# Four stages' starts and attention's score banks in one graph transformer kernel

## The reference, cut to what matters

```python
x = x + gnn0(ln(x), adj)      # 8 heads of 16: softmax(mask(n n^T / 4)) n, then an MLP 128 -> 512 -> 128
x = x + ffn0(ln(x))           # slice attention: 64 slices per head, attention among them, and back
x = x + gnn1(ln(x), adj)      # two graph convolutions: root and relation weights, divided by the degree, elu
x = x + ffn1(ln(x))           # shared expert, plus the best 2 of 8 experts per token

# gnn0, per graph
normed = layer_norm(x, gamma1, beta1)
qkv = normed.reshape(b_, n_, H, HD).transpose(0, 2, 1, 3)
scores = jnp.einsum('bhqd,bhkd->bhqk', qkv, qkv) * scale
attn = jax.nn.softmax(jnp.where(adj_matrix[:, None, :, :] > 0, scores, -jnp.inf), axis=-1)
out = jnp.einsum('bhqk,bhkd->bhqd', attn, qkv)
```

## Time and profile before

| | us |
|---|---|
| median of 3 runs | 2728.17 (2725.9 to 2731.24) |
| the profiled execution, and its span | 2732.5, 2730.6 |
| TensorE busy | 2636.5 (97%) |
| VectorE, GpSimd, ScalarE busy | 1928.5, 1499.3, 1471.2 (71%, 55%, 54%) |
| attention, MLP, slice attention, graph stage, experts | 536.5, 237.5, 762, 538.5, 656.5 |

### The profile page before, as it was taken

How to read it: one execution, slowest core, us unless ns; L and a number is a source line. 1 busy time by engine, 2 the same in 40 slices (tenths; PEclk the granted TensorE clock), 3 DMA queues, 4 the chain that set the end, 5 groups by cost and what they waited for, 6 DMA issues and landing times. The chain is left out here.

```text
span 2730.6 us, 85746 instructions
## 1 busy us (share of the span) xinstructions
PE 2636.5 (97%) x28783; PEld 2141.0 (78%) x28784; DVE 1928.5 (71%) x6630; ACT 1471.2 (54%) x2930; POOL 1499.3 (55%) x2542
## 2 busy tenths in 40 slices
PE   8999999899989999999999899899998999999999
PEld 4666666589968888888888677777788999999888
DVE  5777777567779999999999588777864544555453
ACT  2555555455547777777767455444553444444444
POOL 5555555333335555555555367676752666666664
PEclk8999999999999999999999999999999999999999
DMA  1111111000000000000000011111511222222264
GB/s 53 32 35 35 35 31 44 10 0 0 0 2 1 0 0 0 0 0 0 0 0 1 25 53 59 55 52 56 161 64 46 77 77 77 77 77 77 81 200 139
DMA packets 158118, 118.26 MB, mean 43 GB/s; under 512 B 20151, under 2 KB 145594, under 8 KB 158011
## 3 DMA queue, kind: packets, MB, share of 16 engines
q1 hardware_dynamic: 140602, 81.02, 10.7%
q0 software_dynamic: 17408, 35.95, 3.9%
HBM read 68.36 MB, written 48.56 MB: 43 GB/s over the span
## 5 line engine op out<-in xcount | busy, mean ns | idle before, releaser
L2027 POOL DMA_INDIRECT token_y<-e_y,e_rows x288 | 295.7, 1027 | 78.8 <-issue 76.6
L2070 ACT ACTIVATE e_hidden<-e_ps,e_b1g 128x512 f32<-128x512 f32 x288 | 194.6, 688 | 258.8 <-PE e_ps L90 258.1
L1303 POOL DMA_INDIRECT sorted_z<-r_z,r_rows x256 | 264.3, 1032 | 67.1 <-issue 63.9
L2122 PE MATMUL e_ps<-expert_w,e_hidden 128*128 x2304 | 280.3, 275 | 0.0
L2122 PEld LDWEIGHTS e_ps<-expert_w,e_hidden 128*128 128x128 f32 x2304 | 273.9, 192 | 6.3
L514 DVE TENSOR_REDUCE a_V<-a_ps_s 128x8 f32<-128x1024 f32 x128 | 156.9, 1226 | 131.0 <-PE a_ps_s L394 131.0
L842 POOL TENSOR_TENSOR s_share<-s_att,s_rsum 128x256 f32<-128x256 f32 x128 | 78.7, 615 | 309.5 <-DVE s_rsum L1117 309.5
L2199 DVE TENSOR_TENSOR e_biased<-e_ps,expert_b 128x512 f32<-128x512 f32 x72 | 49.8, 692 | 213.8 <-PE e_ps L2122 213.8
L394 PE MATMUL a_ps_s<-a_nT 16*128 16x128 f32 x2048 | 186.0, 300 | 0.1
L402 PE MATMUL a_ps_st<-a_topT,a_nT 17*128 17x128 f32 x2048 | 184.7, 298 | 0.1
L394 PEld LDWEIGHTS a_ps_s<-a_nT 16*128 16x128 f32 x2048 | 136.5, 188 | 45.8 <-issue 45.5
(11 more groups left out here) (400 smaller groups left out, 8123.8 us busy)
## 6 DMA issues: line engine op xcount, KB each, us to landing
e_z<-sorted_z SPq DMA_DIRECT2D x72, 260.0 KB
c_y<-token_y SPq DMA_DIRECT2D x22, 512.0 KB, 4.2
X<-in_x_dram SPq DMA_DIRECT2D x32, 256.0 KB, 2.8
a_adj<-in_adj_dram SPq DMA_DIRECT2D x32, 256.0 KB, 2.8
g_adj<-in_adj_dram SPq DMA_DIRECT2D x32, 256.0 KB, 2.9
out_dram<-X SPq DMA_DIRECT2D x32, 256.0 KB, 2.5
c_y_s<-token_y SPq DMA_DIRECT2D x10, 512.0 KB, 4.9
token_y<-e_y,e_rows POOLq DMA_INDIRECT x288
```

What stands on the lines that cost most here:

```text
L1303: nc.gpsimd.indirect_dma_start(sh.sorted_z, bass.IndirectOffsetOnAxis(ap=rows[own][:, e * GB + piece:e * GB + piece + 1], axis=0), zr[own] ...
L2027: nc.gpsimd.indirect_dma_start(sh.token_y, bass.IndirectOffsetOnAxis(ap=rows[p][:, b:b + 1], axis=0), y[p][:, b, :], None).then_inc(y_scat ...
L2070: nc.scalar.activation(hidden[p][:, c, :], ps_1[c % 2][:, :], ACT.Gelu, bias=b1g[p][:, c:c + 1]).then_inc(s["hidden_done"], 1)
L2122: last = nc.tensor.matmul(ps_2[q][:, b, :], hidden[q][:, f, b * T:(b + 1) * T], w2[:, bass.ds(e, 1), f * D:(f + 1) * D].squeeze(1), start= ...
```

## The change

In attention the buffers are exchanged: `ps_s` gets two, `ps_st` one. The mask of the first scores moves ahead of that of the second and waits neither for `top_done` nor for nT; the second's waits for the exponential of the graph before (k - 2 where it was k - 3); the wait for nT stands ahead of the score products. Products on the identity (`drained`, `keep_warm`), whose results nobody reads, are added: in attention's last steps 1, 3, 2 and 2, behind them 5; in the MLP 5 ahead of the constants' products, 4 behind their first part, 9 and 7 ahead of the second stage of steps 2 and 3, 8 at the end; in slice attention 6 at the start and 4 behind the transposes of steps 1 to 4; in the graph stage 8 remain of 24. The weights' preparation goes into VectorE's steps 0, 1 and 2 of the MLP, their split halves with it. Slice attention's SP loads the graph stage's weights and first two adjacency groups, and its GpSimd makes the constants, a part per step. The graph stage's SP loads the experts' first two groups of rows once plan and scatters are there, and its VectorE adds the expert biases in the last step.

Some buffers become shared for it; the two halves of the two weights serve later stages as `zTh` and `zTl`. The diff, cut to its core:

```diff
-        ps_s, ps_st = ps("a_ps_s", [T, 2, 4, T]), [ps(f"a_ps_st{i}", [T, 2, 4, T]) for i in range(2)]
+        ps_s, ps_st = [ps(f"a_ps_s{i}", [T, 2, 4, T]) for i in range(2)], ps("a_ps_st", [T, 2, 4, T])
...
+            def drained(count):
+                for i in range(count):
+                    nc.tensor.matmul(ps_s[i % 2][:, 0, :, :], sh.ident_bf[:, :],
+                                     sh.ident_bf[:, :].unsqueeze(1).to_broadcast([T, 4, T]), start=True, stop=True)
...
-                    if live(kk, 2, n_graphs):
-                        own, i = (p, b - 2) if b >= 2 else (q, b + 2)
-                        if since(kk, 4):
-                            pe.wait_ge(s["prob_done"], k - 3)
-                        for c in range(2):
-                            nc.tensor.matmul(ps_st[b % 2][:, c, :, :], edge_bias[own][:, i, :],
-                                             sh.ident_bf[:, :].unsqueeze(1).to_broadcast([T, 4, T]),
-                                             start=True, stop=False)
                     if live(kk, 0, n_graphs):
                         if b == 0:
                             pe.wait_ge(s["bias_done"], t - 1)
-                        pe.wait_ge(s["nT_done"], k + 1)
-                        if since(kk, 1):
-                            pe.wait_ge(s["top_done"], k)
                         for c in range(2):
-                            nc.tensor.matmul(ps_s[:, c, :, :], sh.ident_bf[:, :],
+                            nc.tensor.matmul(ps_s[b % 2][:, c, :, :], sh.ident_bf[:, :],
                                              edge_bias[p][:, b:b + 1, :].to_broadcast([T, 4, T]),
                                              start=True, stop=False)
+                    if live(kk, 2, n_graphs):
+                        own, i = (p, b - 2) if b >= 2 else (q, b + 2)
+                        if since(kk, 3):
+                            pe.wait_ge(s["prob_done"], k - 2)
+                        for c in range(2):
+                            nc.tensor.matmul(ps_st[:, c, :, :], edge_bias[own][:, i, :],
+                                             sh.ident_bf[:, :].unsqueeze(1).to_broadcast([T, 4, T]),
+                                             start=True, stop=False)
                     if live(kk, 4, n_graphs):
+                        if kk is not None and kk > n_graphs:
+                            drained({1: 1, 2: 3, 3: 2}[kk - n_graphs])
...
+                    if live(kk, 0, n_graphs):
+                        pe.wait_ge(s["nT_done"], k + 1)
...
+            drained(5)
...
+            keep_warm(0, 5)
             pe.wait_ge(center_step, 3)
...
             last.then_inc(late_turned, 1)
+            keep_warm(0, 4)
...
+                            if known in (2, 3):
+                                keep_warm(p, 9 if known == 2 else 7)
                             pe.wait_ge(yT_split, t - 1)
...
+                if part == 0:
+                    dve.wait_ge(late_made, 4)
+                    nc.vector.tensor_copy(sh.wfx[:, :], ps_f)
...
+                if part == 1:
+                    nc.vector.tensor_copy(sh.wfx[0:1, :], sh.frow[:, :])
...
+                    for (high, low), whole in pairs:
+                        last = nc.vector.tensor_copy(high[:, :], whole[:, :])
+                    after(last)
+                if part == 2:
+                    for (high, low), whole in pairs:
+                        nc.vector.tensor_tensor(low[:, :], whole[:, :], high[:, :], ALU.subtract)
...
+                if known is not None and known < 3:
+                    weights(known)
                 if known == groups:
-                    weights_and_biases()
+                    biases()
...
+            for tile, a in loads:
+                sp.dma_start(tile[:, :], a, allow_slow_non_contiguous=True).then_inc(s["next_loaded"], 16)
+            for i in range(2):
+                sp.dma_start(sh.g_adj[i][:, :, :], adj_g[i]).then_inc(s["next_loaded"], 16)
...
+                if 2 <= part < 6:
+                    nc.gpsimd.memset(sh.filler[:, 2 * part - 4:2 * part - 2, :, :], 0.0).then_inc(s["next_made"], 1)
...
+                step(t, r, k, known)
+                if known is not None and known <= 6:
+                    next_constants(known)
...
+            keep_warm(6)
             pe.wait_ge(s["constants"], 1)
-            pe.wait_ge(s["weights_split"], 2)
...
+                    if known is not None and known <= 4:
+                        keep_warm(4)
...
-            keep_warm(24)
-            pe.wait_ge(s["w_loaded"], 80)
-            pe.wait_ge(s["before_set"], 2)
-            pe.wait_ge(s["ones_set"], 1)
+            keep_warm(8)
...
+            sp.wait_ge(planned, 1)
+            for i in range(4):
+                sp.wait_ge(scattered[i], groups // 4 * 2 * GB * 16)
+            for i in range(2):
+                start = nc.sync.value_load(sh.plan[0:1, 1, i:i + 1], min_val=0, max_val=EXPERTS * (capacity + W) - W)
+                sp.dma_start(sh.routed_z[i][:, :, :], sh.sorted_z[bass.ds(start, W), :].rearrange("(b p) d -> p b d", p=T))\
+                  .then_inc(first_loaded, 16)
...
+                elif u == EARLY + 2:
+                    dve.wait_ge(s["experts_loaded"], 16 * (4 + FC))
+                    nc.vector.tensor_tensor(sh.expert_b2[:, :, :], sh.expert_b2[:, :, :],
+                                            sh.shared_b2[:, :].unsqueeze(1).to_broadcast([T, EXPERTS, D]),
+                                            ALU.add).then_inc(b2_added, 1)
```

More of the change, by code:

```diff
@@ L621, in _, with keep_warm @@
         def _(pe):
+            def keep_warm(own, count):
+                for i in range(count):
+                    nc.tensor.matmul(ps_2[own][:, :, :], sh.ident_bf[:, :],
+                                     sh.ident_bf[:, :].unsqueeze(1).to_broadcast([T, GB, T]), start=True, stop=True)
+            keep_warm(0, 5)
             pe.wait_ge(center_step, 3)
@@ L672, in _ @@
             run_steps(pe, step, groups, LAG, PEEL)
+            for i in range(8):
+                nc.tensor.matmul(ps_1[i % 2][:, :], sh.ident_bf[:, :],
+                                 sh.ident_bf[:, :].unsqueeze(1).to_broadcast([T, GB, T]), start=True, stop=True)
         @block.vector
```

185 lines of the change are left out of this document (94 added, 91 removed).

## The result

The changed kernel takes 2700.57 us (median of 4 runs, 2692.53 to 2706.44), the kernel before beside it 2728.41: ratio 0.9896, 95% interval 0.9864 to 0.9927. Six more runs of it gave 2696.30 against 2729.03, ratio 0.9877 (0.9851 to 0.9902). The forecast was 2696.4. The ten times spread over 31 us (2689.42 to 2720.65), those of the kernel before, measured beside them, over 11 (2724.57 to 2735.23), in a later round over 18 (2724.33 to 2742.8).

The account below looks back on a forecast made before the run. Attention is bound by TensorE, which waits 0.21 us per graph for VectorE's maximum. Terms -22 + 0.5 - 0.5 - 3.0 - 3.8 - 3.0 = -31.8 us take 2728.2 to 2696.4 us; range 2684 to 2718.

Parts of the forecast that it names:

- The banks: Attention: exchanged banks and mask order remove TensorE's wait for VectorE's maximum; 0.18 us in each of 122 graphs, 22 us less.
- Attention's end: Last three graphs: second mask stands behind the exponential, ahead of the copy's transposes; with fillers 0.5 us more, 0 to 1.5.
- Rival D: Attention: exponential starts later, so the second mask waits for ScalarE in every graph and the kernel is slower; chance 0.03.
- Rival B: Attention: the exponential takes the maximum's place, so the banks gain nothing and 10 us remain, 2718; chance 0.14.
- The MLP's start: First group 2.6 us earlier, nearly all given back to VectorE's weights in the fill; 0.5 us less, 3 less to 3 more.
- The slice stage's start: Weight halves gone from VectorE's front, 2.0 us, and fillers holding the clock, 1.0; 3.0 us less, 1 to 4.5.
- The graph stage's start: Weights and adjacency loaded a stage earlier, transposes 4.6 us earlier, minus 0.8 for the clock; 3.8 us less, 2 to 5.
- the first products would run before the clock is back: Graph stage's start: with 8 fillers for 24, the first products run at the lower clock; cost 0.8 us.
- The experts' start: Bias sum and first two token loads moved into the graph stage, first product earlier; 3.0 us less, 2 to 3.5.
- Rival C: Borders give nothing: earlier starts wait for the next late thing, or the clock falls elsewhere; 2707, chance 0.14.
- some us either way: Graph stage: the clock may fall at other moments, changing the time by some us in either direction.
- The sum: Whole kernel: -22 + 0.5 - 0.5 - 3.0 - 3.8 - 3.0 = -31.8 us, giving 2696.4 us.

Follow-up runs that it names:

- e1: The kernel before with only the exchange of attention banks and the mask order, no fillers, other stages as before: 2706.76 us against 2729.03, ratio 0.9917.
- e9: The changed kernel with the two score masks in the other order, second mask first: 2743.29 us, ratio 1.0084 to the kernel before.
- e6: The changed kernel with the MLP's weight preparation and splits back at the MLP's end, constants' products still early: 2688.70 us, ratio 0.9839.
- e5: The changed kernel without its added fillers in attention's end, MLP and slice stage, the graph stage's eight kept: 2700.80 us, ratio 0.9887.
- e2: The changed kernel with attention as before (banks, order, no filler there), so the borders' part alone: 2726.24 us, ratio 0.9990.
- e7: The changed kernel with 21 more filler products in the last 10 us of the slice stage: 2691.15 us, ratio 0.9862.
- e8: The changed kernel with 21 fillers in the slice stage's end and three for one before each graph-stage r_z wait: 2683.44 us, ratio 0.9825.
- e10: The changed kernel with the expert bias sum back in front of the experts' stage, early token loads kept: 2702.85 us, ratio 0.9895.

## Why the prediction was right, and where it was not

**The banks, -22.** Right in mechanism and size: 22.3 by the times of e1, 23.8 by the two profiles (a first half-clock stretch of 17.1 for 20.5 us is the difference, half of it 1.7). The period is 3.69 us as composed, the mean 3.72. Attention's end, which I gave 0.5 us more, took 0.9 more (from the last graph's first mask to the MLP's start 16.66 us, 15.78 before); e1 without fillers has 16.61, so they are not the cause. Rival D did not come true, but had its place right: with the order turned the exponential costs 0.40 in each graph (e9), where the prediction's figures give 209.15 - 208.75 = 0.40.

**Rival B** falls with e1. The Trainium skill (TensorE: Matmul & The Clock Gate, "HAM oscillation — how this bites in real kernels") reports that adding PSUM double-buffering gave its kernel no further gain. This case differs from that one: here it was worth 22 us (e1), where VectorE's maximum on the bank stood ahead of a mask in each period.

**The MLP's start, -0.5.** 0.6 at the last product (235.1 to 234.5), near the forecast by luck, as the comparison below shows. The reason given, VectorE's weights in the fill, is shown by e6 (2.8 us worse than at the end), and the clock's part by e5 (2.6). One reading was wrong: the row at 562.00 in the earlier trace rows is the second half of the second group, not a third group; it came 0.37 us earlier, forecast 0.1. And the comparison flatters the change: from attention's end to the slice stage's first logits the old code took 242.7 us in before and 239.8 in e1, the new code 240.2 in after and 241.9 in e2. With other stretches of half clock in the MLP the same code differs by more than the term: the MLP's and slice stage's starts together are worth anything from 2.5 us less to 2.2 us more.

**The slice stage's start, -3.0.** From the stage's first instruction on VectorE 2.1 us at the first logits, the 2.0 of the splits, and 2.4 from the eighth graph's on to the last (41.61 to 39.25, 735.4 to 733.0). The fillers' part of it is shown by e5: 1.7 us are lost without them, where I had 1.0. But the parts do not add: with the splits early and no fillers, e5 keeps 0.7 us or less of the 2.0.

**The graph stage's start, -3.8.** Here lies the step that failed. The transposes came 4.7 us earlier (forecast 4.6), in seven other profiles 3.7, where the eight fillers at half clock held them. And I priced "the first products would run before the clock is back" at 0.8 us, and by the fourth transposes it was 4.2, so 0.5 us were left. I had looked at the clock behind the border and not at the stage before: it empties with waits of 0.4 to 3.1 us, and the 24 fillers of the earlier trace rows, which I counted as a cost removed, had run through the half-clock stretch ahead of the first products (3.4 us, over at 1540.8). No run puts the 24 back, so that they would have helped is argued. What is shown is the way with the stage's end filled: e7 gives 3.0 us back, e8 4.7.

The whole stretch, from the slice stage's first logits to the graph stage's fourth transposes, over all profiles: 794.5 and 794.3 us with the old code (before, e1), 790.4 to 797.7 in seven with the changed code (after 793.6) and 798.2 in e5, 1.7 of it from the slice stage's start, 789.0 to 790.5 in the four with the 21 fillers. The 790.4 is e9, where the border's stretch was 3.4 us and over 0.1 us ahead of the first transposes: there the term is kept in full. So the early start alone gave anything from 4 us less to 3 us more; with the clock held at the border it gave 3.8 to 5.5 in each of four.

**The experts' start, -3.0.** 3.2, of which e10 shows 1.3 to be the bias sum. The last 1.7 us to the end were not forecast. The half-clock stretch behind that border was 6.8 us long for 10.2, but e1, with the old code and 6.8 us too, took 648.3 us for before's 649.3 and after's 647.5: about half is the clock, the other half stays open.

**The rest of the graph stage.** My text allowed "some us either way", and it was +4.6 us. From the fourth transposes to the last shared product it took, with one filler at the wait, 489.4 to 503.5 us in the eight profiles that have the changed code there, 498.9 and 498.0 with the old; with three fillers 485.5 to 486.0 in four profiles. So the change did not break this stage, it moved it within a spread that an idle wait per group leaves open. What sets the places of the stretches stays open.

**The sum**, -31.8, was 27.5 in the profiles; by the times 27.8 and 32.7. Attention was forecast at two thirds of it and is nearly nine tenths; of the borders' 10.3 us e2 found 2.8. That the total came out within 4.2 us of the forecast is in part luck: attention gave what it was to give, the borders' parts largely cancelled, and the runs vary by more than the error. Rival C, at 0.14, was closer to what happened than I made it: the borders gave their time at their place and lost most of it again, C's second reason.

## What to carry to other kernels

Exchange buffers between two waits only together with the order: put the work that needs no wait ahead of the one that now has it, and check in the rows that its length covers the release. A start made earlier is worth what is left of it some groups later, so read the granted clock on both sides of a border, from where the stage before runs empty, and compare several groups in, not at the first product. Fillers ahead of work that could start hold it up when they run at half clock. Where TensorE waits once per iteration and the clock sits a little below 1.00, fillers in just that wait (0.4 us more in a wait of 0.4 us in the mean and 0.6 at most) gained 9 us and narrowed the spread here. A part of a change worth 1 or 2 us should be judged by its stretch in the profile, never by the total.

## What was unexpected of the hardware

- One idle stretch of 2.99 us at 17 us of the run was followed by half the clock for 17.1 us in one execution and 54.6 in another of the same program, though TensorE was busy without a gap from 37 to 75 us in both (38.00 of 38 us). With it filled five executions lay within 0.52 us of each other; the same kernel with the stretch left empty had spread over 3.1, the changed kernel over 31.
- With three products of 0.21 us for one in a wait, the granted clock of a stage of 500 us went from 0.96 to 1.00, though that wait had been 0.6 us at most.
- In the two profiles of the changed kernel, and in that of e10, which is the same until the end of that stage, the first seven half-clock stretches of the graph stage behind the border's stood at the same distances from its first transposes within 0.2 us (26.1 to 319.6), although attention differed by up to 17 us; the second of them, at 108.0, stood elsewhere with the old attention (94.8 in e2) or the masks' other order (146.7 in e9), without the fillers (121.5 in e5) and with a filled slice end (118.8 in e7), but not with another MLP (107.9 in e6, where the first three were the same). The first stood at 25.9 to 26.5 in all of these but e7 (23.2) and e9 (none).
